# Where a fused decoder kernel projects its cross-attention keys and values, and when the next group's recurrence runs

## The reference

```python
x = _layernorm(x + rwkv_block(x))                 # time mixing with a recurrence, channel mixing
x = _layernorm(x + gated_memory_attention(x, ctx))
x = _layernorm(x + top1_mixture(x))               # 8 experts
x = _layernorm(x + strided_sparse_attention(x))   # 16 heads of 8
x = _layernorm(x + cross_attention(x, ctx, ctx))  # 16 heads of 64
x = _layernorm(x + top2_mixture(x))               # 8 experts, 2 per token, capacity 40
# cross attention
Q, K, V = x @ Wq.T + bq, ctx @ Wk.T + bk, ctx @ Wv.T + bv
out = softmax(Q @ K.T / 8) @ V @ Wo
# recurrence over the tokens, per feature: w = -exp(time_decay), u = time_first
no  = max(o, u + kt);  out = (exp(o - no) * p + exp(u + kt - no) * vt) / (exp(o - no) * q + exp(u + kt - no))
no2 = max(o + w, kt);  p, q = exp(o + w - no2) * p + exp(kt - no2) * vt, exp(o + w - no2) * q + exp(kt - no2)
```

## Time and profile before

| | |
|---|---|
| median of 3 runs | 1443.53 us |
| the profiled execution | 1442.27 us |
| its span in the trace | 1440.5 us |
| busy: PE, PE weight loads | 1228.9 us (85%), 800.9 us (56%) |
| busy: DVE, ACT, POOL | 763.2 us (53%), 678.5 us (47%), 156.5 us (11%) |
| mean granted PE clock | 0.925 of full |
| DMA over the span | 10 GB/s, nearly all of it in the first 70 us |

### The profile page before, as it was taken

One profiled execution on the slowest core, in us unless ns is written; L12 is line 12 of the kernel. 1 busy time (PEld: TensorE's weight loads), 2 busy tenths in 40 slices (PEclk: granted clock), 3 DMA queues, 4 the chain that ended last, 5 costly groups with the idle time before them and its releaser, 6 DMA issues.

```text
span 1440.5 us, 21943 instructions
## 1 busy us (share of the span) xinstructions
PE 1228.9 (85%) x7355; PEld 800.9 (56%) x7355; DVE 763.2 (53%) x1906; ACT 678.5 (47%) x1850; POOL 156.5 (11%) x272
## 2 busy tenths in 40 slices
PE   3789989995788898999498989899849898899967
PEld 2564755553665485555375458455537647655536
DVE  6532655568533375557743246555774326555551
ACT  3341765553433285555244147555515506655533
POOL 4300210002010120000211012000021102100000
PEclk8799999997789999999688999999959999999988
DMA  7200000000000000000001000000000000000000
GB/s 238 71 16 0 0 1 1 1 1 1 1 18 15 0 0 1 1 1 1 1 1 32 1 0 1 1 1 1 1 1 1 8 0 0 1 1 1 1 0 8
DMA packets 21059, 15.53 MB, mean 11 GB/s; under 512 B 872, under 2 KB 18646, under 8 KB 20958
## 3 DMA queue, kind: packets, MB, share of 16 engines
q1 hardware_dynamic: 20958, 14.24, 3.4%
HBM read 13.18 MB, written 1.05 MB: 10 GB/s over the span
## 4 chain that ended last, share of the span: by engine, by line
issue 78%; PE 11%; POOL 5%; DVE 2%; POOLq 2%; ACT 1%; SPq 1%; DVEq 0%; DMA 0%; ACTq 0%
PE ps L746 4%; POOL rstd L1390 3%; PE ps L766 2%; PE ps L754 2%; POOLq L1389 1%; PE ps L742 1%; PE ps L728 1%; SPq L425 1%; POOL nTok L1429 0%; PE ps L729 0%; DVE snm L1749 0%; POOL rms_inv L1390 0%; PE ps L538 0%; ACT arena L1194 0%; POOL big L1407 0%
## 5 line engine op out<-in xcount | busy, mean ns | idle before, releaser
L1047 ACT ACTIVATE arena<-ps 128x512 f32<-128x512 f32 (+7 forms) x304 | 171.1, 573 | 312.4 <-PE ps L841 228.0
L1825 DVE TENSOR_REDUCE nmax<-ps 128x1 f32<-128x512 f32 x256 | 164.6, 686 | 138.5 <-PE ps L830 138.5
L1225 ACT ACTIVATE arena<-ps,nmax 128x512 f32<-128x512 f32 x256 | 174.6, 686 | 8.0 <-DVE nmax L1825 8.0
L841 PE MATMUL ps<-ident,arena 128*128 128x128 f32 x1024 | 149.4, 282 | 22.7 <-ACT arena L1225 22.6
L841 PEld LDWEIGHTS ps<-ident,arena 128*128 128x128 f32 x1024 | 110.0, 141 | 104.2 <-issue 63.1
L1830 DVE COPY arena<-ps 128x512 f32<-128x512 f32 x128 | 87.9, 687 | 75.5 <-PE ps L841 75.5
L678 PE MATMUL ps<-big,w1a 128*128 128x512 f32 x256 | 117.3, 603 | 2.9 <-DVE big L1715 2.9
L1388 POOL TENSOR_TENSOR vare<-mv,eps_ln 128x2 f32<-128x2 f32 x64 | 13.9, 217 | 809.0 <-DVE mv L1501 808.5
L1194 ACT ACTIVATE arena<-ps,snm 128x136 f32<-128x136 f32 x256 | 91.7, 374 | 6.3 <-DVE snm L1749 6.3
L678 PEld LDWEIGHTS ps<-big,w1a 128*128 128x128 f32 x256 | 46.4, 190 | 61.2 <-issue 60.1
L710 PEld LDWEIGHTS ps<-xwT,ctxT 128*128 128x128 f32 x512 | 66.6, 203 | 20.9 <-issue 9.9
(11 more groups left out here) (316 smaller groups left out, 2191.8 us busy)
## 6 DMA issues: line engine op xcount, KB each, us to landing
ctx<-in_ctx_dram SPq DMA_DIRECT2D x4, 512.0 KB, 3.6
w1a<-in_L_ffn_W_dram SPq DMA_DIRECT2D x1, 2048.0 KB, 10.0
w1b<-in_L_ffn_W_dram SPq DMA_DIRECT2D x1, 2048.0 KB, 11.4
w2b<-in_L_ffn_W_dram SPq DMA_DIRECT2D x8, 256.0 KB, 6.4
X<-in_x_dram SPq DMA_DIRECT2D x4, 256.0 KB, 2.8
out_dram<-Y SPq DMA_DIRECT2D x4, 256.0 KB, 2.3
arena<-in_L_xattn_Wq_dram SPq DMA_DIRECT2D x1, 512.0 KB
arena<-in_L_xattn_Wk_dram SPq DMA_DIRECT2D x1, 512.0 KB
```

The costliest lines, as they stand in the source:

```text
L841: last = pe.transpose(ps[:, 4 + h, k * P:(k + 1) * P], cprob[:, h, k * P:(k + 1) * P], ident[:, :])
L1047: return act.activation(dst, src, ACT.Copy)
L1225: act.activation(cprob[:, h, :], bank(2 * (t % 2) + h), ACT.Exp, bias=nmax[:, s:s + 1], accum_out=rsum[:, j % 2, s:s + 1]).then_inc(c_exp, 1)
L1825: dve.tensor_reduce(nmax[:, s:s + 1], bank(s % 4), AX.X, ALU.max, negate=True)\
```

## The change

All 32 projections of a group are made outside the pair loop. Every pair has four homes of its own (keys and values of either sequence), in buffers that are not in use at that time: the arena, `big`, `big2`, `kv_more`, and also X0, `ctx`, V, `rf`, `nTok`, `alpha`, qT, kT, OT, nT and qpT. The order is now a table for keys and one for values. Per group: pair 5's four projections stand in the routing of the mixture before (behind a `turn_ctx` that has moved there from the mixture's end); pair 6's four at the start of `memory`; 6 at the end of `memory`; 4 instead of 3 in the start of `mixture_top1`; 9 instead of 6 at its end; 5 instead of 6 at the end of `sparse_attention`; none in the loop. In the prologue `turn_ctx` and pair 5's projections stand around the second turn of the tokens. The next recurrence runs one pair sooner: its moments and its key mix in pair 5, its value mix and first exponents in pair 6, its sums inside pair 7; its denominator stands at the head of the routing, its inverse behind the routing, and `rec_attend` behind the first expert instead of ahead of it. The loads of the next x and context wait for pair 3's values (X0 and `ctx` are homes of pair 3).

```diff
+K_ORDER = ((5, 0), (5, 1), (6, 0), (6, 1), (7, 0), (7, 1), (0, 0), (0, 1), (2, 0), (3, 0),
+           (1, 0), (1, 1), (4, 0), (4, 1), (2, 1), (3, 1))
+V_ORDER = ((5, 0), (5, 1), (6, 0), (6, 1), (7, 0), (7, 1), (0, 0), (0, 1),
+           (1, 0), (1, 1), (4, 0), (4, 1), (3, 0), (2, 0), (2, 1), (3, 1))
...
@@ SP, in the loop
-                sp.wait_ge(layer_done, it * (LAYERS * GROUP) + GROUP)
+                sp.wait_ge(o_ps, it * PAIRS + 4)
                 load_x(it + 1)
-                sp.wait_ge(av_ps, it + 1)
                 load_ctx(it + 1)
...
@@ PE, memory
+                for seq in range(GROUP):
+                    project_k(6, 2 + seq, seq)
                 turn_x(it, 1, 1, wait=False)
+                for seq in range(GROUP):
+                    project_v(6, 4 + seq, seq)
+                keys_read(it, 6, 1)
                 pe.wait_ge(xw_ready, it + 1)
...
@@ PE, the pair loop
-                    if t == 1 and j + 1 == PAIRS and more_groups:
-                        pe.wait_ge(kvr_ready, (it + 1) * 3 + 1)
-                        rec_project(it + 1, 1, 7)
-                    if t == 2 and j in LATE:
+                    if t == 2 and j == PAIRS - 2 and more_groups:
                         pe.wait_ge(wo_added, it * (PAIRS + 1) + j + 1)
-                        project_k(LATE[j], 7, 0)
-                    if t == 3 and j in LATE:
-                        keys_read(it, LATE[j], 1)
-                        project_v(LATE[j], 7, 0)
+                        rec_project(it + 1, 0, 7)
...
@@ PE, mixture_top2
                 last.then_inc(r1_ps, 1)
+                if more:
+                    turn_ctx(it + 1, 5)
+                    for seq in range(GROUP):
+                        pe.wait_ge(ctxT_ready, (it + 1) * 2 + seq + 1)
+                        project_k(5, 3 + seq, seq)
                 pe.wait_ge(two_hot, it + 1)
...
                 last.then_inc(pos_ps, 1)
+                if more:
+                    for seq in range(GROUP):
+                        project_v(5, seq, seq)
+                    keys_read(it + 1, 5, 1)
                 pe.wait_ge(disp_ready, it + 1)
...
                 if more:
-                    rec_attend(it + 1)
+                    values_read(it + 1, 5, 1)
                 up(0)
                 for e in range(E):
                     if e + 1 < E:
                         up(e + 1)
                     down(e)
+                    if more and e == 0:
+                        rec_attend(it + 1)
...
-                if more:
-                    turn_ctx(it + 1, it)
...
@@ ACT, mixture_top2
                 x_turned(it, 5)
+                if more:
+                    rec_receptance(it + 1, 7)
+                    ctx_turned(it + 1, 5)
                 act.wait_ge(e1_arg, it + 1)
                 act.activation(ex1[:, :, :], ex1[:, :, :], ACT.Exp).then_inc(e1_exp, 1)
                 if more:
-                    rec_receptance(it + 1, 7)
+                    for seq in range(GROUP):
+                        keys(it + 1, 5, 3 + seq, seq)
+                    for seq in range(GROUP):
+                        context_values(it + 1, 5, seq, seq)
...
@@ DVE, the pair loop and behind it
-                        if j == PAIRS - 2 and more_groups:
+                        if j == PAIRS - 3 and more_groups:
                             if t == 0:
                                 rec_first_moments(it + 1)
                             if t == 1:
                                 rec_first_normalised(it + 1)
                             if t == 3:
                                 rec_key_mix(it + 1)
+                        if j == PAIRS - 2 and more_groups:
+                            if t == 0:
+                                rec_value_mix()
+                            if t == 3:
+                                rec_exponents(it + 1, 0)
+                                rec_exponents(it + 1, 1)
                         if j == PAIRS - 1 and more_groups:
                             if t == 0:
-                                rec_value_mix()
-                            if t >= 2:
-                                rec_exponents(it + 1, 2 * t - 4)
-                                rec_exponents(it + 1, 2 * t - 3)
+                                rec_exponents(it + 1, 2)
+                            if t == 1:
+                                rec_exponents(it + 1, 3)
+                            if t == 2:
+                                rec_sums(it + 1)
...
-                if more_groups:
-                    rec_sums(it + 1)
-                    rec_denominator(it + 1)
-                    rec_inverse(0)
                 normalise(PAIRS - 1)
-                if more_groups:
-                    rec_inverse(1)
...
@@ DVE, mixture_top2: ahead of the router's logits, and behind the combining weights
+                if more:
+                    rec_denominator(it + 1)
                 dve.wait_ge(r1_ps, it + 1)
...
                 if more:
+                    for b in range(GROUP):
+                        rec_inverse(b)
                     rec_wkv(it + 1)
```

267 lines of the change are left out of this document (131 added, 136 removed).

## The result

The changed kernel takes 1358.0 us (median of 4 runs, 1350.95 to 1363.1) against 1443.39 us of the kernel before, run beside it: a ratio of 0.9404, 95% interval 0.9371 to 0.9437. I had said 1379, so it is 21 us faster than forecast, at the very edge of my range (1358 to 1404) and nearest to the rival in which the fill keeps the clock up (1354). The profiled execution took 1359.2 us, its span is 1357.5, and the mean granted clock rose from 0.925 to 0.962.

What follows compares the result with a forecast made beforehand. PE was taken to set the pace of a late pair. The eight parts summed to -64.2 us, taking 1442.3 to 1378.1; 1.3 for the median made 1379 us, range 1358 to 1404.

Steps and rivals of the forecast that it cites:

- the fill keeps the clock up: Rival: in routing, memory start and top-1 start and end the clock never falls, as PE is hardly idle; 1354 us, chance 0.20.
- Late projections: Pair loop: twelve late projections leave, 3.41 us for each of three late pairs in four groups; -40.9 us.
- The recurrence sooner: Pairs 5 to 7 and way to X: recurrence one pair sooner, 42.9 against 49.3 us; -6.4 a group, -19.3 in all.
- The routing: Routing: transposes and four projections fill PE's idle time around the positions; +0.5 us a group, +1.5 in all.
- the low case: Routing: at 1.2 GHz the added work takes 10.5 us for 6.7 idle, and the gather starts some 3.6 late.
- Memory: Memory stage's start: pair 6's four projections are covered by waits, the clock may gain; -1.5 us for three seams, -4.5.
- Top-1 start: Start of top-1 mixture: four projections for three, at 0.66 of the clock; +1.2 us a group, +4.8 in all.
- Sparse start: Top-1 end: three more projections in idle time, sparse attention's first matmuls gain from the clock; -1.2 us a group, -4.8.
- The end of the sparse attention: Sparse attention's end: one projection fewer, for which X had waited; -0.75 us a group, -3.0 in all.
- Prologue: Prologue: `turn_ctx`, its copy and two key projections stand ahead of the tokens' second turn; +2.0 us (0 to 5).
- paid for at half clock: Rival: routing, memory start and top-1 start and end at their upper bounds, +28 us; 1407 us, chance 0.14.

## Why the prediction was right or wrong

The sign, the bound and the order of the parts were right; the sum was 19 us short in size.

1. **Late projections.** -40.7 against -40.9, and the run without them won 41.7. Reading the price off a neighbouring pair that lacks the work was sound.
2. **The recurrence sooner.** The waits at the two spreads (0.73, 1.92) and the way to X (6.44) came as forecast. The step that failed is "Pair 7 keeps the receptance projection (1.0) on top of the fourth group's 13.7", with the wait of 1.5 behind it: both measured about nothing. I added PE's work to a pair in which PE is not the bound: it has no scores of a next pair to do, and waits for copies and exponentials, also in the group from which I took 13.7 (1.36 and 0.78 us). The projection went into the first of these waits, the scans lengthened the second by 0.13; twice the projection's work on top cost 0.6 to 0.7. One group of the three took 14.8, at the lower clock, which I had not allowed for. And I sized the scans by a row in which POOL worked beside them (2.30, now 1.26). With pair 6 at 18.6 for my 19.5 (its two projections show as 0.9, not 1.7), this is 8.6 us.
3. **The routing.** +0.8 against +1.5. The gather is 0.7 late (I said 0.9; my 10.5 for 6.7 in the low case would make 3.8, not 3.6); from its start to the recurrence's second turn 1.9 us are won, mostly by the gather itself at the higher clock (2.39 for 4.64). The late start and 4.6 us in all behind the second turn give that back; 2.8 of these stand ahead of the third group's memory layer, where the clock fell early. The added table switches left the logits-to-gather time at 6.47 in the kernel with the recurrence's places alone, below the 7.02 of before, so no drain shows on the path. ACT's second load of tables ends at 696.62 in that kernel, and the exponentials start at 696.74.
4. **Memory.** -6.8 against -4.5, and that it is this near is luck. By group it is -1.4, +0.4, -5.9 and +0.1: one layer beyond my bound of -3.5, two with nothing, and a first group that I had not counted. The run without the fill showed that the fill is worth 8.3 us here.
5. **Top-1 start.** -0.1 against +5.2. The cost was right and the clock was not: where the clock is as before, one projection more costs 1.2 us (group 2, 0.66) and 1.3 (group 4, 0.83). The step that failed is to give this to all four groups, with the clock's gain ("At best [...] -0.9") put at nothing: it rose in the other two (0.66 to 1.00 and to 0.83), and they came out 2.2 and 0.4 us shorter.
6. **Sparse start.** -12.2 against -8.2 for parts 6 and 7. "Gain up to 1.6 if the clock stays up", of which I took 1.2: it stayed up in all four groups, and was worth some 2.2 (3.0 a group, less 0.9 for part 7). The run with six projections gave 2.7 to 3.0 back.
7. **The end of the sparse attention.** It has no run of its own; groups with the same low clock at their start give 0.7 to 0.9 us for the one projection, against 0.75.
8. **Prologue.** +2.2 against +2.0.

The rival "the fill keeps the clock up" has the right time by partly the right reason: the clock goes with some 12 us of the miss, not with all of it, and only sparse attention kept it in every group. The rival "paid for at half clock" fell by the routing (0.82). I gave the clock 0.20 where the trace had said that all low stretches follow idle time that the change was about to fill; that deserved more.

## What to carry to other kernels

Before adding a moved instruction's duration to a stretch, ask who ends the waits in it: where the engine waits for others behind the new place, the addition can go into those waits, and twice the work is a cheap test of that. When two instances of a stretch differ in time, look at their granted clocks first. Price fills by what they do to the next stretch as well: removing work made this kernel slower three times (by 6 to 11 us). A wait split in two by real work went with a clock as high as with a fill and cost nothing; a fill of the wait's full length is paid in every group whose wait is shorter. One trace of a clock that changes from group to group is one draw: count it over the traces before calling it the work of an edit.
